# Output projection, norm/router/quantise chain and FFN: five stages with barriers, or one stage batch by batch

## The chip, the cores and the metric

The kernel runs on one core of a Trainium2 chip. The metric is the device time of one execution in microseconds (us). Five engines work from queues of their own, in order: TensorE (PE in the profile, its weight loads PEld), VectorE (DVE), ScalarE (ACT), GpSimd (POOL) and SyncE (SP), which here issues all DMAs. They meet only at semaphores.

## The reference

Four blocks, each added to the residual x of shape (2, 512, 1024), each on a layer norm of x, in float32:

```
x = x + attention(norm(x), context) @ wo        # 32 query heads of 128, wo: 4096 x 1024
n = norm(x)                                     # router
s = softmax(n @ router_w.T + router_b)          # 64 experts
top = top_k(s, 8); w = s where it is in top, else 0
x = x + n * sum(top) + w @ expert_b
n = norm(x)                                     # quantised product
q(v, s, z) = (clip(round(v / s + z), 0, 255) - z) * s
x = x + q(n, s1, z1) @ q(context, s2, z2)       # context: 1024 x 1024 for each batch
n = norm(x)                                     # FFN on NF4 weights
x = x + (silu(n @ d1.T) * (n @ d2.T)) @ d3.T    # d1, d2: 2752 x 1024, d3: 1024 x 2752
```

d1, d2 and d3 are w1, w2 and w3 after NF4: each block of 64 values is divided by its largest magnitude, moved to the nearest of 16 code values, and multiplied back.

## The kernel before

The 1024 tokens (2 batches of 512) are eight tiles of 128. Full-precision products are made of three matmuls (`split_matmul`, L116): a float32 operand is split into a high part (`F32R`, an ACT copy) and the low rest (a subtraction), and high x high, high x low and low x high are summed in PSUM.

The program is a row of stages, each an `nc.Block()` of its own; between two stages all engines wait for each other. The front stage (projections q, k, v) and the attention stage end with the attention's heads in DRAM (`o_d`), and have prepared a part of the NF4 weights on the side. From there on:

- `output_stage` (L1232): a loop of passes over 8 heads. The heads and their rows of `wo` are loaded whole (128 x 1024), ACT makes the high parts, POOL the low parts (L1340, L1342; DVE those of the first four heads, L1368, L1370). PE sums four heads in PSUM for each of 16 output tiles of 128 x 512; DVE adds every one of these partial sums to `X` (L1380): 128 sums.
- `norm_stage` (L302), `router_stage` (L1416), `norm_stage`, `quantised_stage` (L1555), `norm_stage`: the chain, over all 1024 tokens in each step. The third norm also transposes and splits the tokens into `yT_h` and `yT_l`.
- `ffn_stage` (L1707): a loop over 22 chunks of 128 hidden rows. Weight rows come from DRAM (`ff_raw`), PE transposes them in halves of 4 x 128 columns (L1919), ACT makes the high part (L1982), DVE the low part (L2023). For each chunk PE makes gate and up for both batches (L118 to L120, tiles `ff_g`), ACT and DVE make silu(gate) * up and its split (L1987, L2030, L1991, L2035); for each pair of chunks PE multiplies down (`ff_y`), and DVE adds to `X` (L2041): 176 sums.

NF4 weights are prepared in units of 128 x 1024 (`Nf4`, L123): DVE finds the block maxima (L193 to L200), POOL scales (L205), ACT makes 15 times a tile `above` that is large where the value is over a code boundary (L213), DVE takes 15 times the minimum of it and the code's step and adds it to `val` (L224 the first, L228 the others), POOL multiplies back (L233), SP stores. The steps are written by hand between the other work of the queues. The output stage does 16 units, the FFN stage 17. `above` lies in PSUM in the front and output stages (`above_in_psum=True`) and in SBUF in the FFN stage, where PSUM is full.

Of the kernel before, what the change touches and what calls it, by code (L numbers as in the profile page):

```python
# [299 lines left out]


def norm_stage(nc, tag, X, ident, xT=None, xn_all=None):  # L302


    with ExitStack() as ctx:
        sb, ps, sem, event = make_tools(ctx, nc, tag)
        st = sb("st", [P, TT, 2, 6], F32)
        mv = sb("mv", [P, TT, 2], F32)
        s = sb("s", [P, 5, TT], F32)
        xn = xn_all if xn_all is not None else sb("xn", [P, 2, D], F32)  # L310
        slots = TT if xn_all is not None else 2
        seq, var_ready, root_ready, normed = sem("seq"), sem("var"), sem("root"), sem("normed")
        turned, hi_out, lo_out = sem("turned"), sem("hi"), sem("lo")
        if xT is not None:
            tp = ps("tp", [P, 2, DC, P])
        block = ctx.enter_context(nc.Block())

        @block.scalar
        def _(act):
            act.wait_ge(var_ready, 1)  # L320
            act.activation(s[:, 1, :], s[:, 0, :], ACT.Sqrt).then_inc(root_ready, 1)
            if xT is not None:
                for t in range(TT):
                    act.wait_ge(turned, t + 1)
                    act.activation(xT[0][:, :, t * P:(t + 1) * P], tp[:, t % 2], ACT.Copy).then_inc(hi_out, 1)

        @block.vector
        def _(dve):
            steps = [0]

            def after(ins):

                steps[0] += 1
                ins.then_inc(seq, 1)
                dve.wait_ge(seq, steps[0])

            for t in range(TT):
                for h in range(2):
                    last = dve.bn_stats(st[:, t, h, :], X[:, t, h * 512:(h + 1) * 512])
            after(last)  # L340
            for t in range(TT):
                last = dve.bn_aggr(mv[:, t, :], st[:, t, :, :].rearrange("p a b -> p (a b)"))
            after(last)
            dve.tensor_scalar(s[:, 0, :], mv[:, :, 1], EPS, None, ALU.add).then_inc(var_ready, 1)

            dve.wait_ge(root_ready, 1)
            after(dve.reciprocal(s[:, 2, :], s[:, 1, :]))
            after(dve.tensor_tensor(s[:, 3, :], s[:, 0, :], s[:, 2, :], ALU.mult))
            after(dve.tensor_tensor(s[:, 3, :], s[:, 3, :], s[:, 1, :], ALU.add))
            after(dve.tensor_scalar(s[:, 2, :], s[:, 3, :], 0.5, None, ALU.mult))  # L350
            after(dve.reciprocal(s[:, 4, :], s[:, 2, :]))

            def norm(t):
                if xT is not None and t >= 2:
                    dve.wait_ge(turned, t - 1)
                dve.tensor_scalar(xn[:, t % slots, :], X[:, t, :], mv[:, t, 0:1], s[:, 4, t:t + 1],
                                  ALU.subtract, ALU.mult).then_inc(normed, 1)

            def low(t):
                dve.wait_ge(hi_out, t + 1)  # L360
                sl = slice(t * P, (t + 1) * P)
# [1809 lines left out]
```

## Time and profile before

Median of three runs 3216.23 us (3208.83 to 3219.86). The profiled execution's span, from its first to its last instruction, is 3214.7 us, 1.5 us under that median; no other time of that execution is given. Mean granted TensorE clock 0.957.

| Stretch | from, to (us) | length |
|---|---|---|
| front and attention | 0 to 1708 | 1708 |
| output stage | 1708 to 2138 | 430 |
| chain: norm, router, norm, quantise, norm | 2138 to 2397 | 259 |
| FFN | 2397 to 3215 | 818 |

| Engine | busy (us) | share of the span |
|---|---|---|
| PE (matmuls) | 2970.7 | 92% |
| PEld (weight loads) | 2400.8 | 75% |
| DVE | 2596.9 | 81% |
| ACT | 2112.6 | 66% |
| POOL | 1036.4 | 32% |

A row of a timeline is one instruction: start, duration, engine, line, operation, the tile written and the tiles read, and in brackets how long the engine was idle before and who released it. A duration contains whatever an instruction waits for after its start. Matmuls overlap: a duration of 0.39 us does not mean that the next one starts 0.39 us later. A granted clock of 1.00 is 2.4 GHz, 0.50 is 1.2 GHz.

### The profile page before, as it was taken

The page shows a single profiled execution, that of the slowest core. Times are in us where ns is not written, and L with a number is a line of the kernel's source. Part 1 is how long each engine was busy: PE and PEld are TensorE (multiplying, and loading weights), DVE is VectorE, ACT ScalarE, POOL GpSimd, SP SyncE. Part 2 cuts the span into 40 slices and gives each one's busy share as a digit, 9 for nine tenths or more (in the row PEclk, how much of TensorE's full clock was granted, in tenths as well). Part 3 has the DMA queues.
Part 4 walks back from the last instruction along what each step waited for, and adds up shares of the span by engine and source line. Part 5 has one row for each costly group of instructions (what it writes and reads, how often), then busy time and mean ns, then how long its engine had stood idle before and what let it go on. Part 6 is the DMA issues. An engine that isn't in the chain of part 4 may idle for free. (4 is left out here: it accounts for less than half of the span.)

```text
span 3214.7 us, 41676 instructions
## 1 busy us (share of the span) xinstructions
PE 2970.7 (92%) x14140; PEld 2400.8 (75%) x14144; DVE 2596.9 (81%) x3708; ACT 2112.6 (66%) x2759; POOL 1036.4 (32%) x615
## 2 busy tenths in 40 slices
PE   7999999998999999999997999948369999999999
PEld 6888788886888888888885667735147777777787
DVE  5999999986888888888885999984866888888753
ACT  4786767766888788888885888842415555555521
...
GB/s 174 147 162 177 118 114 140 148 119 144 70 92 83 63 96 80 79 83 80 89 50 193 125 136 124 98 33 1 105 40 73 66 72 66 72 82 70 66 40 56
DMA packets 188441, 307.37 MB, mean 96 GB/s; under 512 B 15712, under 2 KB 102752, under 8 KB 188256
## 3 DMA queue, kind: packets, MB, share of 16 engines
...
q14 instruction: 92, 0.75, 0.1%
...
## 5 line engine op out<-in xcount | busy, mean ns | idle before, releaser
L213 ACT ACTIVATE fr_nf_above<-fr_nf_raw,sharp 128x1024 f32<-128x1024 f32 (+1 forms) x360 | 390.0, 1098 | 127.9 <-DVE fr_nf_val L228 115.7
L228 DVE SCALAR_TENSOR_TENSOR fr_nf_val<-fr_nf_above,fr_nf_val 128x1024 f32<-128x1024 f32 (+1 forms) x336 | 402.7, 1199 | 34.2 <-ACT fr_nf_above L213 9.1
L1141 DVE CUSTOM_DVE_ANT_0 at_sc<-at_s,at_mk 128x1024 f32<-128x1024 f32 x256 | 312.1, 1219 | 118.0 <-issue 115.4
L1103 ACT ACTIVATE at_pth<-at_t 128x512 fp32r<-128x512 f32 x512 | 277.3, 594 | 119.9 <-PE at_t L1203 119.4
L213 ACT ACTIVATE ff_nf_above<-ff_nf_raw,sharp 128x1024 f32<-128x1024 f32 x255 | 291.7, 1148 | 95.3 <-DVE ff_nf_val L228 72.9
L1156 DVE TENSOR_TENSOR at_ptl<-at_t,at_pth 128x512 fp32r<-128x512 f32 x512 | 327.0, 680 | 19.4 <-ACT at_pth L1103 18.9
L228 DVE SCALAR_TENSOR_TENSOR ff_nf_val<-ff_nf_above,ff_nf_val 128x1024 f32<-128x1024 f32 x238 | 303.5, 1275 | 20.4 <-ACT ff_nf_above L213 18.6
L213 ACT ACTIVATE ou_nf_above<-ou_nf_raw,sharp 128x1024 f32<-128x1024 f32 x240 | 267.3, 1117 | 78.6 <-DVE ou_nf_val L228 66.8
L1093 ACT ACTIVATE at_pr<-at_sc,at_low 128x1024 f32<-128x1024 f32 x256 | 295.0, 1152 | 29.4 <-DVE at_low L1141 29.0
L118 PE MATMUL fr_acc<-fr_xh,fr_wh 128*128 128x512 f32 x768 | 301.0, 392 | 7.2 <-POOL fr_wl L747 5.5
L119 PE MATMUL fr_acc<-fr_xl,fr_wh 128*128 128x512 f32 x768 | 300.4, 391 | 0.0
L120 PE MATMUL fr_acc<-fr_xh,fr_wl 128*128 128x512 f32 x768 | 300.2, 391 | 0.0
L118 PE MATMUL ff_g<-yT_h,ff_guh 128*128 128x512 f32 x704 | 286.4, 407 | 0.0
L228 DVE SCALAR_TENSOR_TENSOR ou_nf_val<-ou_nf_above,ou_nf_val 128x1024 f32<-128x1024 f32 x224 | 273.1, 1219 | 8.1 <-DVE ou_nf_val L228 0.5
L120 PE MATMUL ff_g<-yT_h,ff_gul 128*128 128x512 f32 x704 | 276.2, 392 | 0.0
L119 PE MATMUL ff_g<-yT_l,ff_guh 128*128 128x512 f32 x704 | 274.6, 390 | 0.0
L1203 PE MATMUL at_t<-ident,at_pr 128*128 128x128 f32 x2048 | 267.1, 273 | 6.4 <-DVE at_ptl L1156 5.3
L1203 PEld LDWEIGHTS at_t<-ident,at_pr 128*128 128x128 f32 x2048 | 236.8, 140 | 45.6 <-issue 10.8
L205 POOL TENSOR_TENSOR ff_nf_raw<-ff_nf_raw,ff_nf_am 128x1024 f32<-128x1024 f32 x17 | 42.2, 2485 | 685.8 <-DVE ff_nf_am L200 685.8
L118 PE MATMUL ou_acc<-ou_wh,ou_oh 128*128 128x512 f32 x512 | 211.9, 414 | 42.9 <-DVE X L1380 22.3
L118 PE MATMUL at_o<-at_pth,at_vh 128*128 128x512 f32 x512 | 222.2, 434 | 0.2 <-DVE at_ptl L1156 0.2
L118 PE MATMUL at_s<-at_kh,at_qh 128*128 128x512 f32 x512 | 202.3, 395 | 11.0 <-POOL at_ql L1037 11.0
...
## 6 DMA issues: line engine op xcount, KB each, us to landing
ff_raw<-dq SPq DMA_DIRECT2D x63, 512.0 KB, 4.0
fr_raw<-in_L_xattn_wq SPq DMA_DIRECT2D x32, 512.0 KB, 4.5
...
ou_oraw<-o_d SPq DMA_DIRECT2D x32, 512.0 KB, 3.7
ou_wraw<-in_L_xattn_wo SPq DMA_DIRECT2D x32, 512.0 KB, 3.8
```

Source lines behind the costliest of these rows:

```text
L118: pe.matmul(out, w[0], x[0], start=start, stop=False)
L119: pe.matmul(out, w[0], x[1], start=False, stop=False)
L120: return pe.matmul(out, w[1], x[0], start=False, stop=stop)
L205: pool.tensor_tensor(raw, raw, self.am[:, s, 2, 0:width // BLK].unsqueeze(2).broadcast_to((P, width // BLK, BLK)), ALU.mult).then_inc(self ...
L213: act.activation(self.above[:, (s + j) % 2, 0:width], self.raw[:, s, 0:width], ACT.Relu, bias=self.sharp[:, j:j + 1], scale=SHARP).then_in ...
L228: dve.scalar_tensor_tensor(v, above, STEPS[j], v, ALU.min, ALU.add).then_inc(self.stepped.sem, 1)
L1093: act.activation(pr[:, n % 2], sc[:, n % 2], ACT.Exp, bias=low[:, n % 2:n % 2 + 1], scale=-1.0, accum_out=sums[:, h % 2, quarter:quarter + ...
L1103: act.activation(pt[0][:, h % 2, j * HALF:(j + 1) * HALF, (n % QT) * P:(n % QT + 1) * P], t_ps[:, j], ACT.Copy).then_inc(t_hi.sem, 1)
L1141: dve.tensor_tensor_reduce(sc[:, n % 2], s_ps[:, n % 2], mk[:, bb * QT + n % QT], -1.0, -NEG, ALU.add, ALU.min, low[:, n % 2:n % 2 + 1]).t ...
L1156: dve.tensor_tensor(pt[1][sl], t_ps[:, j], f32(pt[0][sl]), ALU.subtract).then_inc(t_lo.sem, 1)
L1203: last = pe.transpose(t_ps[:, j, c, :], pr[:, n % 2, k * P:(k + 1) * P], ident[:])
```

## The change

`output_stage`, `router_stage`, `quantised_stage`, `ffn_stage` and the three calls of `norm_stage` are replaced by one `tail_stage`, fully unrolled, without barriers inside. Its order is a list of 392 slots (`Plan`). A slot is 12 matmuls of PE with 512 columns: one head of one sweep, half of a gate or up tile, or two down tiles. Every engine goes through the slots in the same order, and does in each the work that belongs to it; the semaphores alone tie the engines together.

- Slots 0 to 127, projection in four sweeps: batch 0 columns 0 to 511, batch 0 columns 512 to 1023, then batch 1. In a sweep the 32 heads are summed in four PSUM banks (`pa`), one for each token tile; DVE adds 16 sums to `X` in all. A head's 128 x 512 of `o_d` and of `wo` lie together in a ring of four buffers; ACT makes the high part of both in one operation (128 x 1024), POOL the low part of three heads of four, DVE that of the fourth.
- The chain of batch 0 lies in slots 64 to 111, beside the projection of batch 1; the chain of batch 1 lies in slots 128 to 175, beside the FFN of batch 0 (`Chain`). The context is quantised in slots 3 to 50 and kept in DRAM (`qb_d`); clips are done by POOL.
- The FFN does chunks 0 to 7 for batch 0, then chunks 0 to 7 for batch 1, then chunks 8 to 21 for both: 30 items instead of 22, and 180 transposed weight halves instead of 132. The low parts of weights and of the hidden rows are made by POOL (DVE before); for the weights ACT makes a second copy of the transposed half in SBUF (`whole`), from which POOL subtracts.
- NF4: 12 units in slots 5 to 115, 21 units in slots 179 to 347. `above` lies in SBUF in both.

Counted from the slot lists (steps are NF4 steps of ACT and of DVE):

| Slots | PE work | NF4 steps | unit scalings on POOL | weight halves | other |
|---|---|---|---|---|---|
| 0-4 | 5 heads | 0 | 0 | 0 | 1 context tile |
| 5-50 | 46 heads | 81 | 10 | 0 | 15 context tiles |
| 51-63 | 13 heads | 23 | 3 | 0 | column sums of batch 0 |
| 64-111 | 48 heads | 68 | 9 | 0 | chain of batch 0, 8 sums into X |
| 112-127 | 16 heads | 8 | 1 | 4 | column sums of batch 1 |
| 128-171 | 32 gate halves, 12 down pairs | 0 | 0 | 48 | chain of batch 1 |
| 172-178 | 3 gate halves, 4 down pairs | 0 | 0 | 5 | last links of the chain |
| 179-219 | 29 gate halves, 12 down pairs | 76 | 9 | 43 | |
| 220-347 | 86 gate halves, 42 down pairs | 239 | 31 | 64 | |
| 348-391 | 26 gate halves, 18 down pairs | 0 | 1 | 16 | |

The core of the diff (the removed stages stand above):

```diff
-    def __init__(self, tools, sharp, above_in_psum=False):
+    def __init__(self, tools, sharp, above_in_psum=False, buffers=None):
...
+        if buffers:
+            self.raw, self.val, self.above, self.am = buffers
...
+class Plan:
+    SWEEPS, RING = 2 * B, 4
+    FIRST = SWEEPS * HQ
+    EARLY = 8
+    BASE = (FIRST // 2, FIRST)
+    NI = HC + EARLY
...
+    def halves(self, i):
+        return (0,) if i < self.EARLY else (1,) if i < 2 * self.EARLY else (0, 1)
...
+class Chain:
...
+        r, z, y = [6 + 3 * t for t in range(QT)], [27 + 3 * t for t in range(QT)], [43 + t for t in range(QT)]
...
+def tail_stage(nc, o_d, wo, x, context, scales, router_w, router_b, expert_b, dq, dq3, qb_d, ident, ident_bf, sharp,
+               o_units, f_units, chunk_unit, out):
...
+        pa = ps("pa", [P, 4, 512])
+        pc = ps("pc", [P, 2, 512])
+        pt = ps("pt", [P, 2, 512])
...
+            nf1_buffers = [sb_first(f"nf{k}", [P, 2, D], F32) for k in range(3)] + [am1]
+            ring = sb_first("ring", [P, 4, 2, 512], F32)
...
+        nf1 = Nf4(make_tools(ctx, nc, "t1"), sharp, buffers=nf1_buffers)
+        nf2 = Nf4(make_tools(ctx, nc, "t2"), sharp, buffers=[words(two, 2048 * k, 2048, 2, D) for k in range(3)] + [am2])
...
+        def weight1(q):
+            if q < 5 or q >= FIRST - 12:
+                return 0.0
+            return 2.0 if q < plan.BASE[0] or q >= plan.BASE[0] + 48 else 1.6
...
+            def load_head(q):
...
+                    if k % 4 == 3:
+                        sp.wait_ge(ring_lo_d, k // 4 + 1)
+                    else:
+                        sp.wait_ge(ring_lo_p, k // 4 * 3 + k % 4 + 1)
+                sp.dma_start(ring[:, q % 4, 0], o_d[h][:, b * SQ:(b + 1) * SQ]).then_inc(ring_in[q % 4], 16)
+                sp.dma_start(ring[:, q % 4, 1], wo[h * DH:(h + 1) * DH, n * 512:(n + 1) * 512]).then_inc(ring_in[q % 4], 16)
...
+            def high(q):
...
+                act.activation(ring_h[:, q % 4], ring[:, q % 4], ACT.Copy).then_inc(ring_hi, 1)
...
+            def weight_high(i, xx):
...
+                act.activation(destination(i, xx)[0], pt[:, no % 2], ACT.Copy).then_inc(w_hi, 1)
+                if no:
+                    act.wait_ge(w_lo, no)
+                act.activation(whole[:], pt[:, no % 2], ACT.Copy).then_inc(w_copied, 1)
...
+        def _(dve):
...
+            def low(q):
+                dve.wait_ge(ring_hi, q + 1)
+                dve.tensor_tensor(ring_l[:, q % 4], ring[:, q % 4], f32(ring_h[:, q % 4]), ALU.subtract).then_inc(ring_lo_d, 1)
+
+            def add_heads(w):
+                b, n = divmod(w, 2)
+                for t in range(QT):
...
+                    dve.wait_ge(swept, w * QT + t + 1)
+                    sl = (slice(None), b * QT + t, slice(n * 512, (n + 1) * 512))
+                    dve.tensor_tensor(X[sl], pa[:, t], X[sl], ALU.add).then_inc(o_added, 1)
...
+        def _(pool):
+            def low(q):
+                pool.wait_ge(ring_hi, q + 1)
+                pool.tensor_tensor(ring_l[:, q % 4], ring[:, q % 4], f32(ring_h[:, q % 4]), ALU.subtract).then_inc(ring_lo_p, 1)
+
+            def clip_context(n):
+                pool.wait_ge(ctx_scaled, n + 1)
+                pool.tensor_scalar(rows[:, n % 2], rows[:, n % 2], QMAX, 0.0, ALU.min, ALU.max).then_inc(ctx_clipped, 1)
+
+            def weight_low(i, xx):
+                hi, lo = destination(i, xx)
+                pool.wait_ge(w_copied, plan.turn_no[i, xx] + 1)
+                pool.tensor_tensor(lo, whole[:], f32(hi), ALU.subtract).then_inc(w_lo, 1)
...
+            def hidden_low(i, j):
+                sl = (slice(None), i % 2, slice(j * 512, (j + 1) * 512))
+                pool.wait_ge(h_hi, plan.a_no[i, j] + 1)
+                pool.tensor_tensor(hT[:, 1][sl], hid[:, j], f32(hT[:, 0][sl]), ALU.subtract).then_inc(h_lo, 1)
...
+        def _(pe):
+            def project(w, h):
...
+                for t in range(QT):
+                    if h == 0 and w:
+                        pe.wait_ge(o_added, (w - 1) * QT + t + 1)
+                    last = split_matmul(pe, pa[:, t], [y[:, r, 0, t * P:(t + 1) * P] for y in (ring_h, ring_l)],
+                                        [y[:, r, 1] for y in (ring_h, ring_l)], h == 0, h == HQ - 1)
...
+            for q, slot in enumerate(plan.slots):
+                if slot[0] == "head":
+                    project(*slot[1:])
+                elif slot[0] == "gate":
+                    gate_up(*slot[1:])
+                else:
+                    for k in range(slot[2], slot[2] + 2):
+                        down(slot[1], k)
+                for kind, b, t, h in chain.due("pe", q):
+                    link(kind, b, t, h)
+                for i, xx in plan.turns.get(q, []):
+                    turn(i, xx)
```

## Rows read from the trace of the kernel before

**Rows 1.** Head of the page

```profile
span 3214.7 us, 41676 instructions
```

**Rows 2.** Windows: us, busy of PE, PEld, DVE, ACT, POOL; clock, DMA share, GB/s

```profile
1708.00:2138.00 430.00, 378.59 (x1536) 283.79 (x1536) 391.69 (x422) 328.36 (x305) 193.01 (x88) 0.96 0.37 126
...
2138.00:2397.00 259.00, 132.25 (x541) 84.16 (x546) 167.34 (x321) 65.94 (x83) 2.10 (x2) 0.60 0.14 46
...
2397.00:3215.00 818.00, 794.26 (x3681) 640.64 (x3680) 587.52 (x700) 403.36 (x473) 77.06 (x36) 1.00 0.21 66
```

**Rows 3.** Timeline of PE, output stage: first matmul, one tile to next

```profile
1719.72 0.76 PE L118 MATMUL ou_acc<-ou_wh,ou_oh 128*128 128x512 f32 x1 [11.74 <-DVE ou_wl L1370]
...
1909.80 0.50 PE L118 MATMUL ou_acc<-ou_wh,ou_oh 128*128 128x512 f32 x1
...
1912.78 0.50 PE L118 MATMUL ou_acc<-ou_wh,ou_oh 128*128 128x512 f32 x1
```

**Rows 4.** Timeline of PE, FFN: transposes of one weight half, and after

```profile
2702.61 0.60 PE L1919 MATMUL ff_t<-ident,ff_raw 128*128 128x128 f32 x4
...
2702.96 0.48 PE L118 MATMUL ff_y<-ff_dnh,ff_hh 128*128 128x512 f32 x1
```

**Rows 5.** Timeline of DVE and POOL, FFN: instructions that meet

```profile
2468.84 1.23 DVE L228 SCALAR_TENSOR_TENSOR ff_nf_val<-ff_nf_above,ff_nf_val 128x1024 f32<-128x1024 f32 x1
...
2468.99 2.84 POOL L205 TENSOR_TENSOR ff_nf_raw<-ff_nf_raw,ff_nf_am 128x1024 f32<-128x1024 f32 x1 [66.86 <-DVE ff_nf_am L200]
...
2504.39 2.22 POOL L205 TENSOR_TENSOR ff_nf_raw<-ff_nf_raw,ff_nf_am 128x1024 f32<-128x1024 f32 x1 [30.70 <-DVE ff_nf_am L200]
...
2504.77 2.92 DVE L228 SCALAR_TENSOR_TENSOR ff_nf_val<-ff_nf_above,ff_nf_val 128x1024 f32<-128x1024 f32 x1
...
2507.62 1.27 DVE L2023 TENSOR_TENSOR ff_gul<-ff_t,ff_guh 128x512 fp32r<-128x512 f32 x2
...
2507.78 1.91 POOL L233 TENSOR_TENSOR ff_nf_val<-ff_nf_val,ff_nf_am 128x1024 f32<-128x1024 f32 x1 [1.16 <-DVE ff_nf_val L228]
...
2508.82 1.41 DVE L224 TENSOR_SCALAR ff_nf_val<-ff_nf_above 128x1024 f32<-128x1024 f32 x1
```

**Rows 6.** Tiles: ns min/median/max; NF4 steps and splits on POOL

```profile
L228 DVE SCALAR_TENSOR_TENSOR ou_nf_val<-ou_nf_above,ou_nf_val x224: 1210/1220/1227, 1745.0 to 2139.6; 128x1024 f32<-128x1024 f32 x112
...
L228 DVE SCALAR_TENSOR_TENSOR ff_nf_val<-ff_nf_above,ff_nf_val x238: 1160/1217/2923, 2435.6 to 3099.1; 128x1024 f32<-128x1024 f32 x119
...
L224 DVE TENSOR_SCALAR ff_nf_val<-ff_nf_above x17: 693/1195/1415, 2433.8 to 3036.8; 128x1024 f32<-128x1024 f32 x17
...
L1342 POOL TENSOR_TENSOR ou_wl<-ou_wraw,ou_wh x28: 2390/2412/2436, 1743.5 to 2080.7; 128x1024 fp32r<-128x1024 f32 x28
...
L1037 POOL TENSOR_TENSOR at_ql<-rows,at_qh x64: 1259/1775/2043, 763.2 to 1673.0; 128x512 fp32r<-128x512 f32 x64
```

**Rows 7.** Lines of POOL by form: x count, busy us, mean ns, idle before

```profile
L233 POOL TENSOR_TENSOR ff_nf_val<-ff_nf_val,ff_nf_am 128x1024 f32<-128x1024 f32 x17 | 32.4, 1904 | 75.5 <-DVE ff_nf_val L228 75.5
...
L1908 POOL MEMSET ff_raw<- 128x1024 f32 x1 | 1.0, 952 | 50.9 <-PE ff_t L1919 50.9
```

**Rows 8.** Lines of ACT by form

```profile
L213 ACT ACTIVATE ff_nf_above<-ff_nf_raw,sharp 128x1024 f32<-128x1024 f32 x255 | 291.7, 1148 | 95.3 <-DVE ff_nf_val L228 72.9 <-POOL ff_nf_raw L205 21.4
...
L1318 ACT ACTIVATE ou_wh<-ou_wraw 128x1024 fp32r<-128x1024 f32 x32 | 33.5, 1046 | 1.0 <-DMA ou_wraw<-in_L_xattn_wo 0.9
...
L1982 ACT ACTIVATE ff_guh<-ff_t 128x512 fp32r<-128x512 f32 x88 | 52.2, 593 | 142.4 <-PE ff_t L1919 142.4
```

**Rows 9.** Lines of DVE by form, in norm and router

```profile
L339 DVE BATCH_NORM_STATS2 n_st<-X 128x6 f32<-128x512 f32 x48 | 28.8, 680 | 5.9 <-PEq L1236 5.1 <-PEq L1561 0.4 <-PEq L1418 0.3
...
L356 DVE TENSOR_SCALAR xn<-X,n_mv,n_s 128x1024 f32<-128x1024 f32 x16 | 11.7, 807 | 0.1
...
L1550 DVE SCALAR_TENSOR_TENSOR ro_tmp<-xn,ro_sm,X 128x1024 f32<-128x1024 f32 x8 | 10.2, 1277 | 0.0
```

**Rows 10.** DMA issues of the page: count, KB each, us to landing

```profile
ou_oraw<-o_d SPq DMA_DIRECT2D x32, 512.0 KB, 3.7
```

More of the change, by code:

```diff
@@ L299, in _ @@
             pool.tensor_copy(ident_bf[:], ident[:]).then_inc(made, 1)
[L302 to L361, printed above, removed]
-                dve.tensor_tensor(xT[1][:, :, sl], tp[:, t % 2], f32(xT[0][:, :, sl]), ALU.subtract).then_inc(lo_out, 1)
-            norm(0)
-            for t in range(TT):
-                if t + 1 < TT:
-                    norm(t + 1)
-                if xT is not None:
-                    low(t)
-        if xT is not None:
-            @block.tensor
-            def _(pe):
-                for t in range(TT):
-                    pe.wait_ge(normed, t + 1)
-                    if t >= 2:
-                        pe.wait_ge(lo_out, t - 1)
-                    for c in range(DC):
-                        last = pe.transpose(tp[:, t % 2, c, :], xn[:, t % 2, c * P:(c + 1) * P], ident[:])
-                    last.then_inc(turned, 1)
@@ new lines, in gate, with hidden @@
+            def gate(i, j):
+                a = plan.a_no[i, j]
+                act.wait_ge(gated, plan.gate_no[i, j, 0] + 1)
+                if before(i, j) is not None:
+                    act.wait_ge(gone, plan.a_no[before(i, j), j] + 1)
+                act.activation(act_s[:, j], bank(j, 0), ACT.Silu).then_inc(silu, 1)
+            def hidden(i, j):
+                act.wait_ge(gone, plan.a_no[i, j] + 1)
+                p = i // 2
+                if p and any(t // QT == j for t, n in plan.y_list[p - 1]):
+                    act.wait_ge(y_tiles, plan.y_base[p - 1] + 1 + max(
+                        k for k, (t, n) in enumerate(plan.y_list[p - 1]) if t // QT == j))
+                act.activation(hT[:, 0, i % 2, j * 512:(j + 1) * 512], hid[:, j], ACT.Copy).then_inc(h_hi, 1)
@@ new lines, in _ @@
+            for q in range(2):
+                high(q)
+            for q in range(TOTAL + 2):
+                if q + 2 < FIRST:
+                    high(q + 2)
+                for n in range(NC):
+                    if q == context_slot(n):
+                        scale_context(n)
+                for i, j in plan.gates_done(q - 1, 0):
+                    gate(i, j)
+                for i, xx in plan.turns.get(q - 1, []):
+                    weight_high(i, xx)
+                for i, j in plan.gates_done(q - 1, 1):
+                    hidden(i, j)
+                for kind, b, t, h in chain.due("act", q):
+                    link(kind, b, t, h)
+                for u, j in of1(spread1.steps, q):
+                    nf1.above_scalar(act, u, u % 2, [j])
+                for u, j in of2(spread2.steps, q):
+                    nf2.above_scalar(act, u, u % 2, [j])
@@ L1956, in chunk @@
-            def chunk(pr, m, s, i, first, units):
-                for tile in range(4):
-                    gate_up_tile(m, s, tile)
-                    if s == 0 and tile % 2 == 0 and not (isinstance(pr, int) and pr < 0):
-                        down(pr, tile // 2)
-            def tail(pr):
-                for j in range(2):
-                    down(pr, j)
-            gated.open(pe)
-            tiles.open(pe)
-            for x in range(2, 6):
-                turn(-1, x)
-            program(pe, chunk, tail)
```

1360 lines of the change are left out of this document (682 added, 678 removed).

## The prediction

> **What bounds the kernel now.** The page's head gives the span, 3214.7 us [rows 1]; the median of the runs, 3216.2, is 1.5 above it, so 1.5 is added to a span at the end. Everything up to the attention's end at 1708 stays as it is. The windows by stage come next [rows 2]. In the output stage (430 us) DVE is busy 392 and the TensorE clock is 0.96: DVE bounds it with 16 NF4 units (15 steps each) and 128 sums. In the chain (two norms, router, quantiser, third norm; 259 us) no engine reaches 65%, and the clock is 0.60: it is latency. In the FFN (818 us) PE is busy 794 at 1.00. So two things could be had: most of the 259, and DVE's excess in the output stage.
>
> **TensorE's part.** The first matmul starts 11.7 us after the attention's end, and one tile of 12 matmuls follows the next after 2.98 us [rows 3]. Inside a tile they start 0.23 apart, so 2.73 is work and 0.25 the wait; four transposes take 0.35 and make the matmul behind them start 0.10 late: 0.45 a weight half [rows 4]. I slice the new stage as its program does: one slot is 12 matmuls of 512 columns; slots 0-127 are heads, then gate halves and pairs of down tiles up to 391. A head slot is 2.98; a gate half 2.85 (a wait every two slots), a down slot 3.2 (two waits). 128 heads of 4 x 3 are the 1536 matmuls of before. The FFN's 2112 + 1056 stay too, but as eight chunks are done once for each batch, 180 weight halves are turned, not 132. The chain's own matmuls were 132 us at clock 0.60 [rows 2], so some 40 per batch at full clock. On PE alone: 12 + 128 x 2.98 + 176 x 2.85 + 88 x 3.2 + 180 x 0.45 + 80 = 1338, against 1507 now. Were PE the bound, 169 us would go.
>
> **What the change does to DVE and POOL.** Two edits matter. The NF4 unit's "above" buffer, in PSUM in the output stage, goes to SBUF (`nf1_buffers`, `nf2`). And POOL gets work beside it: three of four head splits, all 180 weight splits (DVE before), all 44 hidden splits (DVE before), and clips. The rows show what happens when a POOL operation meets a DVE operation with two SBUF inputs [rows 5]. POOL starts L205 at 2504.39 and ends at 2506.61; the NF4 step issued at 2504.77 lasts 2.92, and ends 1.08 after POOL. At 2468.99 it is the other way: POOL's 1.90 becomes 2.84 because a step holds until 2470.07. The one-input operation L224 beside L233 lasts 1.41 instead of 0.69, while L2023, which reads PSUM and SBUF, runs through both untouched. The two take turns, whole instruction by whole instruction; the case at 2504.39 recurs eight times. In the output stage, with "above" in PSUM, 224 steps lie between 1.210 and 1.227 beside a POOL that is half busy; in the FFN, with it in SBUF, they reach 2.923 [rows 6].
>
> The Trainium skill ("SBUF — State Buffer", section "Who interferes with whom") says that a DVE instruction with two SBUF inputs, or in a two-port mode, and a GpSimd instruction that reads SBUF hold one pair of ports in turn, for the whole instruction. By that rule the two engines' times add, as in the sums below; without it they lie beside each other, which is the first rival. The trace agrees, with 2.92 for 1.22.
>
> Prices: a DVE step 1.22, the first of a unit 0.69, so 1.185 on average; a split of 128x1024 on POOL 2.41, of 128x512 at least 1.26 [rows 6]; scaling a unit on POOL 1.90; a clip on POOL is in no row: at least a memset, 0.95, at most a split, 2.41; I take 1.90, the in-place product [rows 7]. By the Trainium skill ("GPSIMD Engine Reference", section "4.1 Engine selection") one-input elementwise work there is roughly line-rate, near the memset's 0.95 as an estimate; that would take 18 us off the sum, and no row here shows it. ACT: above 1.15, head split 1.05, weight half 0.59, now twice [rows 8]. Of the chain on DVE, the normalise (0.81) and the gain, priced as a step, take turns with POOL; the statistics (0.68) and all that reads PSUM do not [rows 9].
>
> **The sum, slot by slot.** L = DVE's operations that take turns, G = POOL's, U = DVE's others.
> Slots 0-4: 12 + 5 x 3 = 27 (no steps yet).
> 5-50: L = 81 steps 96 + 11.5 splits 14 + 15 roundings 10 = 120; G = 34.5 splits 83 + 10 scalings 19 + 15 clips 28.5 = 131. Together 251, where PE needs 137 and ACT 157 (46 x 1.05 + 81 x 1.15 + 15 context tiles at 1.05).
> 51-63: L 31 + G 29 = 60.
> 64-111 (first batch's chain): L = 68 steps 81 + 12 splits 15 + 12 normalise, 4 gain, 4 round, 8 sums of products 23 = 119; G = 36 splits 87 + 9 scalings 17 + 4 clips 8 = 112; U = 24 statistics 16, 32 half rows out of PSUM 22, 4 row sums and 4 maxima 12, small ones 12 = 62. How much of U fits beside POOL? In rows 5 about 1.8 of POOL's 5.7 us had such work beside it, 0.31: 35 of 62. So 119 + 112 + 27 = 258.
> 112-127: no steps after 115: 17 + 12 x 2.98 + 4 halves = 55.
> 128-171 (second chain beside the FFN's first batch): PE leads: 32 x 2.85 + 12 x 3.2 + 48 x 0.45 + 40 = 191, with DVE 95 and POOL 76; 9 for hops of the chain that come late: 200.
> 172-178: 27.
> 179-219: L = 76 steps 90; G = 43 + 7 half splits 63, 9 scalings 17: 80; U = 24 sums, 7 products, 5 maxima 30, of which 25 fit: 175 (PE 141).
> 220-347: L = 239 steps 283; G = 64 + 22 half splits 108, 31 scalings 59: 167; U = 82 sums, 22 products, 15 maxima 96, of which 52 fit: 494 (PE 411).
> 348 to the end: 26 x 2.85 + 18 x 3.2 + 16 x 0.45 = 139, and 5 to store: 144.
> Sum 27 + 251 + 60 + 258 + 55 + 200 + 27 + 175 + 494 + 144 = 1691; span 1708 + 1691 = 3399, time 3400: 184 slower. If all of U fits, and a clip is 0.95, it is 1691 - 76 - 18, time 3306; if none of it fits, + 112, time 3512.
>
> **Other edits.** The chain's 259 us do go; their cover are the head and gate matmuls. What is late next is the pair DVE and POOL. Heads are loaded once per batch and half: twice the bytes, 256 issues of 256 KB. A load of twice that size lands in 3.7 us [rows 10], and four ring slots leave it more than two slots of 5 us. With the units, X, the context and its codes' way through DRAM (16 x 512 KB in, 16 x 256 KB out, 2 x 2 MB back) it is some 96 MB in 651 us, 148 GB/s, against 126 at a DMA share of 0.37 in the output stage [rows 2]: nothing. Its wait on SP holds back the context tiles, NF4 units and weights behind it, which then slip with the heads, not further. The 128 sums into X become 16; those 112 x 0.68 = 76 us off DVE are in L and U already. ACT's second copy per weight half (180 x 0.59) waits for POOL's split and holds back silu and "above" behind it; ACT in 179-219 and 220-347 has 147 and 377, under the pair's sums. A chain link on PE that waits holds back the next slot; its links stand one or two slots behind what they need, so I charge only the 9 us above.
>
> **Rivals.** (1) Faster: POOL and DVE lie beside each other, as in the output stage now, because the two seldom meet or the turns are shorter than rows 5. Then each stretch costs its busiest engine: 27 + 157 (ACT) + 43 + 184 + 53 + 200 + 27 + 147 (ACT) + 411 + 144 = 1393, time 3103. For it: POOL had 193 us in the output stage without a trace of it. Against: those steps read PSUM, and every meeting with SBUF in rows 5 shows the turn. It decides as soon as a POOL operation runs inside a step that keeps 1.22.
> (2) The clock falls while heads wait. At half clock a head slot is 2 x 2.73 + 0.25 = 5.7 against 5.5, 4.6 and 5.4 here, and the chain's matmuls double: 46 x 5.7 + 13 x 5.7 + 48 x 5.7 + 80 = 690 for 569, time 3521. For it: 0.60 in the chain now; against: 0.96 in the output stage, where PE also waits [rows 2].
> (3) The chain is not hidden: PE, in order, stands at each link. Half of 259 each time on top of PE's own 143 and 151 makes 272 and 280 for 258 and 200: time 3494. Against: the links' distance.
> (4) Turns and savings cancel: if 0.39 of what the turns add to (1) stays, 3103 + 0.39 x 297 = 3219.
>
> **Chances.** The sum 0.58, clock 0.08, chain 0.09: 0.75 slower. (1) 0.21, faster. (4) 0.04 within 0.3%, about what a measurement can tell from no change. The sum's own range is 3306 to 3512. As (1) with the spread of its sum holds 0.21, a range for 8 in 10 begins inside it: 3120 to 3515.
>
> **What would show it.** NF4 steps in the new stage: their mean over 1.6 us and maxima near 3.6 in slots 5-111, POOL splits stretched over 2.41, head slots of 4.6 to 5.5 us on PE, heads ending near 2360. Wrong if the steps stay near 1.22 and heads end by 2190; (2) if the clock there is under 0.7; (3) if PE's longest waits are on the chain's normalise, pick or round.

## The result, and the profile after

The changed kernel takes 3423.66 us (median of 4 runs, 3423.05 to 3425.37), the kernel before 3215.99 beside it: a ratio of 1.065 (95% interval 1.063 to 1.067), 208 us slower. The forecast was 3400, slower, with a range of 3120 to 3515. The head of the page, to be held against [rows 1], and its busy times:

```profile
span 3423.5 us, 41157 instructions
## 1 busy us (share of the span) xinstructions
PE 3037.4 (89%) x14326; PEld 2465.3 (72%) x14336; DVE 2700.3 (79%) x3463; ACT 2296.4 (67%) x3083; POOL 1559.7 (46%) x904
```

The attention ends at 1708 as before, so the new stage takes 1715.5 us for 1507.

The windows cut the new stage at the starts of the prediction's slots, found on PE's timeline (slots 0-4, 5-50, 51-63, 64-111, 112-127, 128-171, 172-178, 179-219, 220-347, 348 to the end). Columns as in [rows 2]: length, busy of PE, PEld, DVE, ACT, POOL with counts, clock, DMA share, GB/s.

```profile
1708.00:1737.50 29.50, 16.77 (x61) 13.01 (x62) 5.90 (x10) 9.07 (x9) 12.93 (x8) 0.77 0.81 259
1737.50:1962.20 224.70, 152.56 (x557) 113.69 (x555) 212.68 (x125) 148.49 (x141) 153.03 (x62) 0.87 0.61 209
1962.20:2028.70 66.50, 46.09 (x176) 33.85 (x177) 62.27 (x40) 41.76 (x42) 39.05 (x14) 0.88 0.39 138
2028.70:2274.80 246.10, 194.78 (x817) 146.04 (x822) 229.26 (x251) 142.15 (x158) 124.99 (x49) 0.89 0.39 135
2274.80:2328.30 53.50, 50.27 (x225) 38.51 (x224) 28.32 (x21) 26.23 (x30) 34.70 (x15) 1.00 0.41 137
2328.30:2513.50 185.20, 179.16 (x937) 139.71 (x941) 94.92 (x180) 93.30 (x158) 77.91 (x60) 1.00 0.22 69
2513.50:2540.20 26.70, 26.70 (x128) 22.15 (x129) 11.67 (x19) 8.00 (x15) 7.03 (x5) 0.90 0.23 79
2540.20:2742.40 202.20, 158.25 (x668) 125.68 (x666) 137.02 (x120) 130.43 (x173) 97.45 (x58) 0.86 0.24 76
2742.40:3287.80 545.40, 419.43 (x1794) 334.00 (x1793) 439.73 (x392) 356.62 (x416) 214.87 (x121) 0.88 0.19 62
3287.80:3423.50 135.70, 129.38 (x593) 106.32 (x591) 30.43 (x44) 24.51 (x45) 32.66 (x27) 0.99 0.14 49
```

Read it against [rows 2]. The heads end at 2328, where the kernel before had projection and chain behind it at 2397: 69 us earlier, though with only the first batch's chain done. The rest, with the second batch's chain in it, takes 1095 us for the 818 of the FFN before: 277 more. Where PE leads (112-127, 128-171, the end) it is busy nearly throughout and the clock is 0.99 to 1.00. In 5-111 DVE is busy 93 to 95% of the time; a step's busy time contains what it waits for after its start.

What that busy time is made of shows in the tiles (ns min/median/max), the answer to [rows 6] and, for the clip, to the hole in [rows 7]:

```profile
L231 DVE SCALAR_TENSOR_TENSOR tl_nf<-tl_nf x168: 1160/1226/3446, 1747.5 to 2294.0; 128x1024 f32<-128x1024 f32 x168
...
L231 DVE SCALAR_TENSOR_TENSOR tl_two<-tl_two x294: 1159/1226/2743, 2546.4 to 3284.9; 128x1024 f32<-128x1024 f32 x147
...
L1857 POOL TENSOR_TENSOR tl_ring_l<-tl_ring,tl_ring_h x96: 2338/2702/3387, 1716.2 to 2316.5; 128x1024 fp32r<-128x1024 f32 x96
...
L1861 POOL TENSOR_SCALAR tl_rows<-tl_rows x16: 1030/1744/2032, 1738.7 to 1953.5; 128x1024 f32<-128x1024 f32 x16
L1712 DVE TENSOR_SCALAR tl_codes<-tl_rows x16: 632/2614/2889, 1739.8 to 1962.1; 128x1024 bf16<-128x1024 f32 x16
```

The page has their means (busy us, mean ns, idle before):

```profile
L231 DVE SCALAR_TENSOR_TENSOR tl_two<-tl_two 128x1024 f32<-128x1024 f32 x294 | 450.6, 1533 | 124.5 <-ACT tl_two L216 106.5
...
L231 DVE SCALAR_TENSOR_TENSOR tl_nf<-tl_nf 128x1024 f32<-128x1024 f32 x168 | 316.3, 1883 | 22.1 <-ACT tl_nf L216 12.6
```

The steps' median is still 1.226; their maximum is 3.446, and by these means the 462 take 767 us, where at 1.22 they would take 564. Both sides stretch: POOL's splits go from 2.41 to a median of 2.70. One meeting in the heads, DVE's timeline first and then POOL's (start, duration, ..., idle before):

```profile
1810.81 0.63 DVE L1712 TENSOR_SCALAR tl_codes<-tl_rows 128x1024 bf16<-128x1024 f32 x1
1811.36 8.87 DVE L231 SCALAR_TENSOR_TENSOR tl_nf<-tl_nf 128x1024 f32<-128x1024 f32 x4
1820.15 1.22 DVE L1697 TENSOR_TENSOR tl_ring_l<-tl_ring,tl_ring_h 128x1024 fp32r<-128x1024 f32 x1
```

```profile
1810.98 2.22 POOL L208 TENSOR_TENSOR tl_nf<-tl_nf,tl_am 128x1024 f32<-128x1024 f32 x1 [0.40 <-DVE tl_am L203]
1813.16 3.32 POOL L1857 TENSOR_TENSOR tl_ring_l<-tl_ring,tl_ring_h 128x1024 fp32r<-128x1024 f32 x1
```

Four steps need 4.88 alone; they take 8.87. In that stretch POOL does what is left of its scaling (1.84) and one split (2.41 alone, 3.32 here). 4.88 + 1.84 + 2.41 = 9.13: the times add, less 0.26. So these two engines do not meet only at semaphores, as the first section has it: no semaphore ties these steps to POOL's split. And PE, whose tile of 12 began every 2.98 us in [rows 3], now begins them 3.48 and 5.27 us apart here, each time after the head's split:

```profile
1801.88 0.50 PE L118 MATMUL tl_pa<-tl_ring_h 128*128 128x512 f32 x1 [1.09 <-DVE tl_ring_l L1697]
...
1805.36 0.50 PE L118 MATMUL tl_pa<-tl_ring_h 128*128 128x512 f32 x1 [0.46 <-POOL tl_ring_l L1857]
...
1810.63 0.50 PE L118 MATMUL tl_pa<-tl_ring_h 128*128 128x512 f32 x1 [2.26 <-POOL tl_ring_l L1857]
```

The waits (engine, line, waited for: us, times, longest), first of slots 5-50, then of 64-111, then of 220-347:

```profile
ACT tl_nf L216 <- DVE tl_nf L231: 64.1, 39, 4.1
POOL tl_ring_l L1857 <- ACT tl_ring_h L1592: 50.2, 20, 5.2
PEld tl_pa L118 <- POOL tl_ring_l L1857: 48.8, 24, 6.2
...
PEld tl_pa L118 <- DVE tl_ring_l L1697: 20.9, 8, 7.3
...
PE tl_pa L118 <- DVE tl_X L1706: 10.4, 1, 10.4
```

```profile
PE tl_pc L2017 <- DVE tl_two L1796: 16.3, 4, 7.9
PE tl_pa L118 <- DVE tl_X L1706: 14.8, 2, 9.8
...
PE tl_pc L2003 <- DVE tl_two L1767: 12.7, 4, 5.6
```

```profile
POOL tl_gu L1866 <- ACT tl_whole L1613: 118.3, 35, 16.6
PEld tl_pa L118 <- DVE tl_X L1726: 110.9, 20, 12.3
...
ACT tl_two L216 <- DVE tl_two L231: 91.5, 111, 3.0
...
DVE tl_two L231 <- ACT tl_two L216: 60.3, 42, 3.5
```

In slots 5-50 PE waits for a split, by POOL or by DVE, and once, for 10.4 us, for the first sum of a finished sweep of heads (L1706). In 64-111 it waits mostly on the chain, for the rounded row (L1796) and the normalised one (L1767), both DVE's: 45 us of the 246 with the other links. Two more such waits for L1706 are 14.8. In the FFN it waits for DVE's sums into X, which read PSUM and keep their 0.69, but stand in DVE's order behind stretched steps.

### The profile page after: what moved, and what is told of

It reads as the page before. It is cut to its first block, busy times and chain, and to the rows that moved or that the text cites. A ratio compares the mean times of both kernels' runs of the same rounds, so it can differ in the third digit from the quotient of the medians.

```text
span 3423.5 us, 41157 instructions
## 1 busy us (share of the span) xinstructions
PE 3037.4 (89%) x14326; PEld 2465.3 (72%) x14336; DVE 2700.3 (79%) x3463; ACT 2296.4 (67%) x3083; POOL 1559.7 (46%) x904
## 3 DMA queue, kind: packets, MB, share of 16 engines
q1 hardware_dynamic: 230912, 359.63, 31.7%
q8 instruction: 115, 1.88, 0.2%
## 4 chain that ended last, share of the span: by engine, by line
DVE 20%; PE 16%; issue 7%; ACT 5%; POOL 2%; DMA 1%; DVEq 0%; SPq 0%; ACTq 0%
DVE tl_nf L231 7%; DVE tl_two L231 7%; PE tl_pa L118 4%; PE tl_pa L119 3%; PE tl_pa L120 3%; ACT tl_two L216 2%; PE tl_pt L1978 1%; DVE tl_am L196 1%; PE tl_pc L118 1%; PE tl_pc L119 1%; PE tl_pc L120 1%; ACT tl_whole L1613 1%; POOL tl_gu L1866 1%; ACT tl_nf L216 1%; DMA tl_ring<-in_L_xattn_wo 1%
## 5 line engine op out<-in xcount | busy, mean ns | idle before, releaser
L231 DVE SCALAR_TENSOR_TENSOR tl_two<-tl_two 128x1024 f32<-128x1024 f32 x294 | 450.6, 1533 | 124.5 <-ACT tl_two L216 106.5
L216 ACT ACTIVATE tl_two<-tl_two,sharp 128x1024 f32<-128x1024 f32 x315 | 354.4, 1148 | 128.7 <-DVE tl_two L231 109.0
L1857 POOL TENSOR_TENSOR tl_ring_l<-tl_ring,tl_ring_h 128x1024 fp32r<-128x1024 f32 x96 | 265.3, 2769 | 199.9 <-ACT tl_ring_h L1592 199.8
L231 DVE SCALAR_TENSOR_TENSOR tl_nf<-tl_nf 128x1024 f32<-128x1024 f32 x168 | 316.3, 1883 | 22.1 <-ACT tl_nf L216 12.6
L118 PE MATMUL tl_pa<-tl_ring_h 128*128 128x512 f32 x512 | 228.1, 446 | 115.1 <-POOL tl_ring_l L1857 59.1
L1866 POOL TENSOR_TENSOR tl_gu<-tl_whole,tl_gu 128x512 fp32r<-128x512 f32 x120 | 184.4, 1536 | 295.5 <-ACT tl_whole L1613 295.5
L1015 ACT ACTIVATE at_pr<-at_sc,at_low 128x1024 f32<-128x1024 f32 x256 | 295.0, 1153 | 29.7 <-DVE at_low L1063 29.2
L216 ACT ACTIVATE tl_nf<-tl_nf,sharp 128x1024 f32<-128x1024 f32 x180 | 203.9, 1144 | 152.4 <-DVE tl_nf L231 142.3
L118 PE MATMUL tl_pa<-tl_dn,tl_hT 128*128 128x512 f32 x352 | 165.0, 469 | 152.6 <-DVE tl_X L1726 130.5
L964 POOL TENSOR_TENSOR at_ot<-at_ot,at_inv_row 128x512 f32<-128x512 f32 x64 | 87.4, 1366 | 354.3 <-ACT at_ot L1031 354.3
L118 PEld LDWEIGHTS tl_pa<-tl_ring_h 128*128 128x128 f32 x512 | 107.3, 210 | 161.0 <-POOL tl_ring_l L1857 73.9
```

The lines of the kernel that those rows point to most:

```text
L118: pe.matmul(out, w[0], x[0], start=start, stop=False)
L216: act.activation(self.above[:, (s + j) % 2, 0:width], self.raw[:, s, 0:width], ACT.Relu, bias=self.sharp[:, j:j + 1], scale=SHARP).then_in ...
L231: dve.scalar_tensor_tensor(v, above, STEPS[j], v, ALU.min, ALU.add).then_inc(self.stepped.sem, 1)
L1015: act.activation(pr[:, n % 2], sc[:, n % 2], ACT.Exp, bias=low[:, n % 2:n % 2 + 1], scale=-1.0, accum_out=sums[:, h % 2, quarter:quarter + ...
L1857: pool.tensor_tensor(ring_l[:, q % 4], ring[:, q % 4], f32(ring_h[:, q % 4]), ALU.subtract).then_inc(ring_lo_p, 1)
L1866: pool.tensor_tensor(lo, whole[:], f32(hi), ALU.subtract).then_inc(w_lo, 1)
```

## The experiments

Eight kernels: seven edits of the changed kernel and one of the kernel before. The theory is the prediction's: turns of DVE and POOL. The rivals were the loads, the chain's links on PE, the unevenness of DVE's work, and the order of the sums. The slots of all of them, in us (slots 0-4 from 1708, the last to the end of the span; the first column is the prediction's):

| slots | predicted | after | e1 | e2 | e3 | e4 | e6 | e7 | e8 |
|---|---|---|---|---|---|---|---|---|---|
| 0-4 | 27 | 29.5 | 30.2 | 27.9 | 27.3 | 31.7 | 28.5 | 29.7 | 27.8 |
| 5-50 | 251 | 224.8 | 189.0 | 195.9 | 162.8 | 223.8 | 185.5 | 185.5 | 161.5 |
| 51-63 | 60 | 66.5 | 58.1 | 52.8 | 44.2 | 66.5 | 53.8 | 53.8 | 44.2 |
| 64-111 | 258 | 246.1 | 237.0 | 233.7 | 190.1 | 247.9 | 232.1 | 232.0 | 192.7 |
| 112-127 | 55 | 53.5 | 49.4 | 49.4 | 49.4 | 53.2 | 50.6 | 50.1 | 49.4 |
| 128-171 | 200 | 185.2 | 185.1 | 185.1 | 185.2 | 195.2 | 195.1 | 196.6 | 195.1 |
| 172-178 | 27 | 26.8 | 26.7 | 26.9 | 26.9 | 24.1 | 25.7 | 24.1 | 24.1 |
| 179-219 | 175 | 202.1 | 201.9 | 202.2 | 202.2 | 162.3 | 161.4 | 163.7 | 136.2 |
| 220-347 | 494 | 545.5 | 545.5 | 545.5 | 545.5 | 505.3 | 502.2 | 500.8 | 379.4 |
| 348-end | 144 | 135.7 | 135.6 | 135.6 | 135.6 | 133.1 | 133.1 | 132.9 | 132.9 |

**The turns by themselves: one buffer of the kernel before.** e5 takes the output stage's "above" buffer out of PSUM, and changes nothing else: ACT writes it to SBUF, and DVE reads it there.

```diff
-        nf = Nf4(tools, sharp, above_in_psum=True)
+        nf = Nf4(tools, sharp)
```

> The kernel before with one edit: in the output stage 'above' lies in SBUF instead of PSUM. No other instruction changes. Theory (turns): steps 240 x 1.185 = 284, POOL 56 splits x 2.41 + 32 scalings x 1.90 = 196, DVE's others 113, of which 61 lie beside POOL: 284 + 196 + 52 = 532 for a stage of 430; as slots 5-50 came out at 0.9 of such a sum, 480 to 530: time 3265 to 3315. Rival (the changed stage is slow through its own order, not through where the buffer lies): no change, 3215.

Measured: 3340.79 us, ratio to before 1.038 (1.0359 to 1.0402): 122 us slower. The direction is the theory's, the size above its range by 26. The tiles of the output stage, to be held against [rows 6]:

```profile
L228 DVE SCALAR_TENSOR_TENSOR ou_nf_val<-ou_nf_above,ou_nf_val x224: 1207/1225/3312, 1740.3 to 2262.3; 128x1024 f32<-128x1024 f32 x112
...
L1342 POOL TENSOR_TENSOR ou_wl<-ou_wraw,ou_wh x28: 2865/3342/3371, 1739.2 to 2196.1; 128x1024 fp32r<-128x1024 f32 x28
```

The steps' maximum goes from 1.227 to 3.312, and POOL's splits of `wo` from a median of 2.41 to 3.34. The whole cost lies before the last projection matmul, which starts at 2251 for 2129. It is the size of what the steps gain (busy us and mean ns, the kernel before first and then e5): 395.7 - 273.1 = 122.6 us.

```profile
L228 DVE SCALAR_TENSOR_TENSOR ou_nf_val<-ou_nf_above,ou_nf_val 128x1024 f32<-128x1024 f32 x224 | 273.1, 1219 | 8.1 <-DVE ou_nf_val L228 0.5
```

```profile
L228 DVE SCALAR_TENSOR_TENSOR ou_nf_val<-ou_nf_above,ou_nf_val 128x1024 f32<-128x1024 f32 x224 | 395.7, 1767 | 8.1 <-DVE ou_nf_val L228 0.5
```

ACT's 240 operations into the buffer go from 1.117 to 1.150 on average, 8 us in all. In e5's timeline DVE has two steps of 6.13 us together and POOL two splits around them:

```profile
1909.51 6.13 DVE L228 SCALAR_TENSOR_TENSOR ou_nf_val<-ou_nf_above,ou_nf_val 128x1024 f32<-128x1024 f32 x2
```

```profile
1908.40 2.85 POOL L1340 TENSOR_TENSOR ou_ol<-ou_oraw,ou_oh 128x1024 fp32r<-128x1024 f32 x1
1911.22 3.34 POOL L1342 TENSOR_TENSOR ou_wl<-ou_wraw,ou_wh 128x1024 fp32r<-128x1024 f32 x1
```

From 1908.40 to DVE's end at 1915.64 are 7.24 us; two steps of 1.22 and two splits of 2.41 are 7.26. The pieces fit less well than that, since POOL's first 0.59 us lie beside the end of the unit's first step (L224, to 1908.99). The first rival (POOL and DVE lie beside each other) is refuted by one line of code.

**POOL's part in the heads.** e1 gives all 128 head splits to DVE.

```diff
-                if q + 2 < FIRST and (q + 2) % 4 == 3:
+                if q + 2 < FIRST:
                     low(q + 2)
...
-                if q + 2 < FIRST and (q + 2) % 4 != 3:
-                    low(q + 2)
```

> All 128 head splits on DVE (96 of them were on POOL); all else as in the changed kernel (3424 us). Theory (DVE operations with two SBUF inputs and POOL operations take turns, so their times add): a split is 1.22 on DVE and 2.41 on POOL, so each of the 96 moved splits takes 1.2 us off the pair's sum. Slots 5-50: DVE 96 + 56 + 10 = 162, POOL 45, together 207 or less, where 225 was measured: about 190. Slots 64-111: about 230 (246). Heads as a whole about 550 us (620), time about 3350. Rival (DVE, busy 95% of slots 5-50, is simply overloaded, and POOL's work lies beside it): 96 x 1.22 = 117 us more for DVE in the heads, which grow to 700 or more: time about 3500.

Measured: 3372.77, ratio 1.0503 (1.0471 to 1.0535), some 51 us under the changed kernel. Work was added to the busiest engine and the time fell: a split costs DVE 1.22, where on POOL it takes 2.41 of the turns. All of the gain is in slots 0-127; the FFN's slots keep 202 and 545.

**Half of "above" in PSUM.** e2 lays one of the two "above" buffers of the heads' units into `pt`, which is idle there; the other stays in SBUF, so one kernel has both kinds of step beside the same POOL.

```diff
-            nf1_buffers = [sb_first(f"nf{k}", [P, 2, D], F32) for k in range(3)] + [am1]
+            nf1_buffers = [sb_first(f"nf{k}", [P, 2, D], F32) for k in range(2)]
+            nf1_buffers += [[sb_first("nf2", [P, D], F32)[:], pt[:].rearrange("p a b -> p (a b)")], am1]
```

> In the heads' NF4 units one of the two 'above' buffers lies in PSUM (the two banks that the FFN's transposes use from slot 122 on), the other stays in SBUF; the same steps, splits and order. Theory: steps that read PSUM last 1.22 (none over 1.3), steps that read SBUF keep a mean of 1.8 or more; heads shrink by about 65 us, time about 3360. Rival (the steps are long for another reason: queue order, a memory side slower under load): both kinds are alike, time 3400 or more.

Measured: 3366.09 (two runs), ratio 1.0475 (1.0439 to 1.0511). The tile by its source, ACT's operation into PSUM first:

```profile
L219 ACT ACTIVATE tl_pt<-tl_nf,sharp x90: 1095/1107/1122, 1740.4 to 2231.0; 128x1024 f32<-128x1024 f32 x90
L234 DVE SCALAR_TENSOR_TENSOR tl_nf<-tl_pt,tl_nf x84: 1160/1224/1226, 1746.0 to 2233.4; 128x1024 f32<-128x1024 f32 x84
L234 DVE SCALAR_TENSOR_TENSOR tl_nf<-tl_nf x84: 1161/1544/3426, 1747.3 to 2231.1; 128x1024 f32<-128x1024 f32 x84
```

Not one of the 84 steps with an operand in PSUM exceeds 1.226; the 84 in the same units with both in SBUF reach 3.426, with a mean of 1.828. That is the condition of the turn, shown within one execution.

**The heads without steps.** e3 lets steps 1 to 14 of the heads' units work on 64 of 1024 columns, in `above` on ACT and in the step on DVE (that part of the computation is left out).

```diff
-                    nf1.step_vector(dve, u, u % 2, [j], parts1[u])
+                    nf1.step_vector(dve, u, u % 2, [j], parts1[u], 64 if j else D)
```

> In the heads' 12 NF4 units steps 1 to 14 act on 64 of 1024 columns, on ACT and DVE (the values of the other columns are left out); everything else stays. Theory: DVE's side of the pair falls from 120 to about 35 in slots 5-50, so that PE leads there with 46 x 3 = 137 to 150, slots 64-111 with the chain of the first batch need 48 x 2.98 + 40 = 183 to 200, heads about 455 of 620, time about 3260. Rival (3) of the prediction (PE stands at the chain's links): slots 64-111 stay at 230 or more. Rival of the loads (heads are loaded twice): slots 5-50 stay at 200 or more, with PE waiting for the ring's DMAs.

Measured: 3279.1 (one run), and 190 us in slots 64-111, with all of the first batch's chain in them; PE alone needs 48 x 2.98 + 40 = 183. PE's waits on the chain's links are 10 us there instead of 45, with the links where they were: DVE came late to them because of the steps, not because they stand too near. (The cut shortens ACT's part of a step too, so it does not say which of the two engines' parts it was.) So the third rival falls as the cause, though the mark I had named for it (PE's longest waits on normalise, pick or round) is there in the changed kernel. In 5-50 it is 162.8, over the expected 137 to 150: POOL's splits, scalings and clips remain there (busy 127), and PE still waits 23 us for its splits. Waits for a load are 8.9 us in slots 5-50, ACT's.

**The FFN's splits back on DVE.** e4 lets DVE take the weight halves' splits, straight from PSUM, and the hidden halves', from SBUF, so that ACT's second copy goes and POOL keeps only the scalings.

```diff
-                if no:
-                    act.wait_ge(w_lo, no)
-                act.activation(whole[:], pt[:, no % 2], ACT.Copy).then_inc(w_copied, 1)
...
+                dve.tensor_tensor(lo, pt[:, no % 2], f32(hi), ALU.subtract).then_inc(w_lo, 1)
```

> Low parts of weights (180) and hidden rows (44) on DVE, the weights' straight from PSUM, as in the kernel before; ACT's second copy of each weight half goes. Heads unchanged. Theory: a subtraction from PSUM takes no turn with POOL; POOL keeps only the 40 unit scalings in slots 179-347. Slots 220-347: DVE's own 439 and the scalings' turns, about 480 (545 measured); slots 179-219: about 166 (202); time about 3320. Rival (DVE overloaded): 107 x 0.68 + 29 x 0.67 = 92 us more for DVE in slots 179-347, time 3424 to 3500.

Measured: 3353.02, ratio 1.0435 (1.0406 to 1.0463), 71 us under the changed kernel. Slots 179-219 fall to 162 (expected 166), 220-347 only to 505 (expected 480), and 128-171 grow by 10. Slots 220-347, first the window, then the steps' mean and the wait:

```profile
2712.70:3218.00 505.30, 414.32 (x1795) 331.87 (x1794) 445.06 (x479) 323.15 (x349) 73.88 (x32) 0.90 0.21 67
```

```profile
L231 DVE SCALAR_TENSOR_TENSOR tl_two<-tl_two 128x1024 f32<-128x1024 f32 x225 | 296.0, 1315 | 21.5 <-ACT tl_two L216 9.8 <-DVE tl_two L227 0.5
```

```profile
PEld tl_pa L118 <- DVE tl_X L1734: 92.7, 20, 9.9
```

PE still waits 93 us for sums. Unstretched, DVE has 283 + 96 + 64 x 0.68 + 22 x 0.68 = 437 there and POOL 59 of scalings: 496, near the 505. But the two do not stand one behind the other: with a mean of 1.315 the 225 steps hold only 21 us of turns (225 x 0.095), where the changed kernel's 226 have a mean of 1.522 in these slots, 68 us of turns. The rest of the 505 is DVE's own work and 60 us in which it is idle. Nor does e4 show by turns alone where its gain comes from: DVE's waits for ACT's "above" fall from 60.3 to 9.8 us in the same slots, and ACT's second copy, which stood before "above" in ACT's order and waited for POOL's split, is gone as well. No run has the one without the other.

**Both together.** e6 adds to e4 heads' units that work in halves of 512 columns, with both "above" buffers in `pt`.

```diff
-            nf1_buffers = [sb_first(f"nf{k}", [P, 2, D], F32) for k in range(3)] + [am1]
+            nf1_buffers = [sb_first(f"nf{k}", [P, 2, D], F32) for k in range(2)] + [pt, am1]
...
-        nf1 = Nf4(make_tools(ctx, nc, "t1"), sharp, buffers=nf1_buffers)
+        nf1 = HalfNf4(make_tools(ctx, nc, "t1"), sharp, nf1_buffers)
```

> Both mends together: the heads' NF4 steps read 'above' from PSUM throughout (two half-width operations of 512 columns for each step, one bank each, 360 instead of 180), POOL keeps its head splits; FFN splits on DVE as in e4. Theory: in the heads only DVE's splits, roundings and the chain's normalise still take turns. Slots 5-50: DVE 81 x 1.37 + 33 = 144, PE 137, POOL 126: 165 to 175 (225); slots 64-111: 215 (246); heads 510 (620). With e4's 70 in the FFN: time about 3245. Rival (gains overlap, or half-width steps cost more than the turns): 3300 or more.

Measured: 3280.5, ratio 1.0193 (1.0169 to 1.0217): 143 of the 208 us come back, 35 fewer than expected. The turns are gone from the heads' steps, but the halves have a price:

```profile
L1263 ACT ACTIVATE tl_pt<-tl_nf,sharp x360: 665/674/702, 1737.8 to 2223.2; 128x512 f32<-128x512 f32 x180
L1278 DVE SCALAR_TENSOR_TENSOR tl_nf<-tl_pt,tl_nf x336: 628/691/694, 1746.4 to 2223.9; 128x512 f32<-128x512 f32 x168
```

Two halves of "above" take ACT 1.35, where e2's whole one into PSUM has a median of 1.107; two half steps take DVE 1.38 for 1.22. In 5-50 ACT is busy 159 of 185 us, and PE still waits 48 for POOL's splits. Slots 64-111 come to 232, not 215: with the steps' turns gone DVE is still busy 209 there and PE still waits 32 on the chain's links, where e3, with the steps cut, took 190. So DVE's own load, and not the turns alone, makes the links late.

**Is it the unevenness?** e7 is e6 with the FFN steps spread anew: slots of down tiles, where the sums are, get three quarters of a gate slot's share.

```diff
-            return 1.0
+            return 0.75 if s[0] == "down" else 1.0
```

> As e6_psum_ffn, and slots with down tiles get 0.75 of the NF4 steps that gate slots get (it was the same number). In e4's slots 220-347 PE still waits 93 us for DVE's sums into X, which stand behind the steps of their slot: a down slot costs DVE 2 x 0.69 + 1.87 x 1.3 = 3.8, PE 3.2. Theory of uneven slots: with 1.5 and 2.0 steps both kinds cost DVE 3.4; slots 220-347 from 505 to about 480, time 20 to 25 below e6. Rival (DVE's total, 445 of 505, bounds the stretch however it is spread): within 8 us of e6.

Measured: 3277.23, ratio 1.0181 (1.016 to 1.0202), and 500.8 for 502.2 in 220-347. The rival was right: 3 us of time and 1.4 in these slots are no 20, so my reading that DVE's work was only badly spread fell. Only this one spread was tried.

**Is it their total?** e8 is e4 with e3's cut in both sets of units.

```diff
-                    nf2.step_vector(dve, u, u % 2, [j], parts2[u])
+                    nf2.step_vector(dve, u, u % 2, [j], parts2[u], 64 if j else D)
```

> Steps 1 to 14 of all NF4 units of the new stage, heads' and FFN's, work on 64 of 1024 columns (that part of the computation is left out), and the FFN's splits are on DVE as in e4. What is left open by e4 and e7: why slots 220-347 take some 500 us where PE's own sum is 411. Theory (DVE's steps, late by their total, delay the sums into X for which PE waits): without them PE bounds the FFN slots; 179-219 near 145, 220-347 near 415, 128-171 near 185; with the heads' slots as in e3 (163 + 44 + 190 + 49) the stage is some 1382 us, time near 3092, below the 3216 of the kernel before. Rival (the order itself: down tiles wait for the sums of X because two buffers and the slots' order make them, whatever DVE's load): 220-347 stays over 470 and the time over 3140.

Measured: 3053.08 (one run), with 3213.74 for the kernel before beside it. Slots 220-347:

```profile
2539.00:2918.40 379.40, 379.40 (x1795) 312.92 (x1794) 226.81 (x477) 140.28 (x348) 60.05 (x32) 1.00 0.28 90
```

PE is busy without a gap, at clock 1.00, in the same order of the same down tiles: the order is not what holds it, the steps are (ACT's part and DVE's were cut together). From 505.3 to 379.4 go 126 us. It also gives the order's floor for PE, 379 where I had 411, and shows what the one stage takes when its quantising needs next to no time on ACT and DVE: 161 us less than the kernel before with all its steps. What that kernel would take without them was not run, so how much of the 161 is the one stage's is open.

## Why the prediction was right

**The mechanism.** It was forecast from meetings in the FFN before [rows 5] that steps with two SBUF operands and POOL take turns, and that moving "above" to SBUF while POOL gets work makes DVE and POOL one resource. e5 and e2 show the first. e1 shows the second in the heads; in the FFN e4 fits it, but takes ACT's second copy away too. e6 gives back 143 of 208 us by undoing both. The Trainium skill's rule ("SBUF — State Buffer", section "Who interferes with whom") agrees with them: 1.226 at most with an operand in PSUM, 3.426 without. The marks named ahead came as said for the steps' mean in the heads (1.88, over 1.6) and their maximum (3.45, near 3.6), for POOL's splits (median 2.70), and for the slots of 5-111 on PE: 224.8/46 = 4.9, 66.5/13 = 5.1, 246.1/48 = 5.1 for 4.6 to 5.5. The heads ended at 2328, 32 us before the 2360 named.

**The sum** was 1691 for 1715.5, and that it is closer than its terms is luck: slots 5-50 and 64-111 were 38 too dear, 128-171 15, while 179-219 were 27 and 220-347 were 51 too cheap.

- Heads: a clip was taken at 1.90. In e6, where the steps read PSUM, its median is 1.04 (below). For 15 clips that is 13 of the 26 in slots 5-50. For the other 13 I have the overlap at handovers as an estimate: the meeting above lost 0.26 of 9.13, which would be 7 of 251; the rest is open. The Trainium skill ("GPSIMD Engine Reference", section "4.1 Engine selection") calls one-input work on GpSimd "roughly line-rate"; the trace agrees, with 1.04 beside the memset's 0.95 [rows 7].

```profile
L1917 POOL TENSOR_SCALAR tl_rows<-tl_rows x16: 1031/1044/2014, 1737.7 to 1918.0; 128x1024 f32<-128x1024 f32 x16
```

- FFN: the mis-sized term is how much of DVE's other work (sums, products, maxima) fits beside POOL. I took 0.31 of POOL's time from [rows 5]: 25 of 30 in slots 179-219, and 52 of 96 in 220-347. With none it is 200 and 546; measured 202.1 and 545.5. In e4 the same plain sum (496) stands against 505. That fit is no rule: with none, slots 64-111 would be 293, for 246 measured. Why none counts in the FFN isn't settled: single products do run beside a POOL split at 0.68, the steps hold 68 us of turns for POOL's 167, and DVE is idle for some 100 us of the 545, 60 of them waiting for ACT's "above". A step that is late by a turn makes the next "above" late and then the sum for which PE waits; that is the reading that fits, but no run separates it.
- The second chain, 200: 9 us for late hops were not needed, and PE's own part was 6 lower: 185.2, with PE busy 179 at clock 1.00. In 128-171 PE was the bound as said, so a later change there (e4) shows at once as 10 us more.
- The end, 144, was 8 too dear.

**The rivals.** (1) fell to e5. (2): the clock in slots 5-111 is 0.87 to 0.89, not under 0.7; PE's longest single wait in slots 5-50 is 10.4 us, for a sum of a sweep, and its weight load's for a split 7.3. (3) fell to e3 and to slots 128-171, but its mark was badly chosen: a late DVE makes the chain's links late too, so waits on them are common to both causes, and only e3 told them apart. (4) did not come: it needed 0.39 of the 297 us that the turns add, and the time lies 321 above (1)'s 3103. The cover of the loads held: a 256 KB load lands in 3.1 us from `o_d` and 3.9 from `wo`, and the heads move 168 GB/s as a whole, where 148 was the estimate.

**What stays lost.** The best version here with all of its computation, e7, is still 1.8% behind the kernel before. The 259 us of the chain do find cover (in e3 slots 64-111 take 190 with the first batch's chain in them, and 128-171 take 185 with the second's), but the output stage's 379 us of PE and the FFN's 794 had been cover for DVE's 392 and 588 [rows 2]. Without the steps the new order takes 1343 us (e8's whole stage), and the full work of DVE, ACT and POOL has to fit into it. In e4's slots 220-347 DVE is busy 445 us for PE's 379, with 21 of them turns: what is left there is mostly DVE's own load and its waits, and no run parts the two. No version here beats the kernel before.
